# Router weights, value bias and the fourth batch's rows at other places in the head of the first attention

## The reference, cut to what matters

```python
# x (8, 100, 512), context (8, 722, 512) of which the causal mask leaves the first 100 rows
q = layernorm(x) @ q_w + q_b
k = context @ k_w + k_b
v = context @ v_w + v_b                      # 16 heads of 32
y = softmax(mask(q k^T / sqrt(32))) v
x = x + y @ o_w + o_b
# router of the first experts, on layernorm(layernorm(x)) * gamma + beta
logits = xf @ Wg.T + bg                      # 8 experts
```

## Time and profile before

| | us |
|---|---|
| median of 3 runs | 1704.23 |
| lowest, highest | 1703.96, 1705.78 |
| the profiled execution, its own time | 1707.12 |
| span of the profiled execution | 1705.4 |
| PE busy in the span | 1587.5 (93%) |
| DVE, ACT, POOL busy | 1133.0, 821.1, 262.7 |

### The profile page before, as it was taken

How to read it: one execution, slowest core, us unless ns; L and a number is a source line. 1 busy time by engine, 2 the same in 40 slices (tenths; PEclk the granted TensorE clock), 3 DMA queues, 4 the chain that set the end, 5 groups by cost and what they waited for, 6 DMA issues and landing times.

```text
span 1705.4 us, 32823 instructions
## 1 busy us (share of the span) xinstructions
PE 1587.5 (93%) x12252; PEld 1398.6 (82%) x12252; DVE 1133.0 (66%) x2066; ACT 821.1 (48%) x1542; POOL 262.7 (15%) x301
## 2 busy tenths in 40 slices
PE   6999699999999699899999999999999869999992
PEld 5787499999999589689888888888888669999991
DVE  3688667777777552367676766767676677776774
ACT  2444355555555332256555554646464434444442
POOL 1112201000000130011111111111111141111213
PEclk9999799999999899999999999999999979999996
DMA  6997366666666534231120111120203046656653
GB/s 188 363 400 255 110 225 228 218 213 204 221 205 215 146 134 174 100 107 37 33 55 24 52 28 48 28 60 20 60 16 100 19 145 220 212 182 217 228 194 89
DMA packets 93595, 246.06 MB, mean 144 GB/s; under 512 B 32646, under 2 KB 39302, under 8 KB 78390
## 3 DMA queue, kind: packets, MB, share of 16 engines
q1 hardware_dynamic: 84278, 223.15, 38.4%
q0 software_dynamic: 9216, 21.53, 5.5%
HBM read 179.14 MB, written 65.50 MB: 143 GB/s over the span
## 4 chain that ended last, share of the span: by engine, by line
PE 49%; DVE 4%; DMA 2%; ACT 1%; issue 1%; SPq 0%; POOL 0%; DVEq 0%; POOLq 0%; ACTq 0%
PE banks L2031 13%; PE banks L1164 10%; PE banks L2092 5%; PE banks L1141 5%; PE banks L2076 4%; PE banks L2065 4%; PE banks L2106 3%; PE banks L2052 3%; DMA token_sums<-e_y,e_dest 1%; DMA a_bo<-bo 1%; PE banks L1133 1%; ACT a_P L2364 0%; DVE a_nmax L2231 0%; DVE a_cl L2209 0%; DVE x_res L1446 0%
## 5 line engine op out<-in xcount | busy, mean ns | idle before, releaser
L2031 PE MATMUL banks<-a_ch,a_wm 128*128 128x362 f32 (+1 forms) x1024 | 284.6, 339 | 5.3 <-DVE a_cl L2209 5.3
L1217 DVE TENSOR_TENSOR e_lo<-e_raw,e_hi 128x2048 fp32r<-128x2048 f32 x97 | 224.4, 2313 | 53.1 <-ACT e_hi L1301 50.7
L1164 PE MATMUL banks<-e_xh,e_hi 128*128 128x256 f32 x768 | 216.6, 282 | 0.0
L1164 PE MATMUL banks<-e_xl,e_hi 128*128 128x256 f32 x768 | 216.1, 281 | 0.0
L1164 PE MATMUL banks<-e_xh,e_lo 128*128 128x256 f32 x768 | 215.8, 281 | 0.0
L1301 ACT CAST e_hi<-e_raw 128x2048 fp32r<-128x2048 f32 x98 | 185.9, 1905 | 13.4 <-PE banks L1141 13.4
L2031 PEld LDWEIGHTS banks<-a_ch,a_wm 128*128 128x128 f32 x1024 | 185.3, 189 | 6.7 <-DVE a_cl L2209 6.4
L2031 PE MATMUL banks<-a_cl,a_wm 128*128 128x362 f32 (+1 forms) x512 | 168.4, 329 | 0.0
L1112 POOL DMA_INDIRECT token_sums<-e_y,e_dest x32 | 76.9, 2404 | 580.8 <-DVE e_y L1274 321.8
L1141 PE MATMUL banks<-e_hi,e_hh 128*128 128x512 f32 x384 | 152.8, 398 | 0.0
L1164 PEld LDWEIGHTS banks<-e_xh,e_hi 128*128 128x128 f32 x768 | 145.2, 189 | 7.7 <-DVE e_lo L1217 2.1
(11 more groups left out here) (296 smaller groups left out, 3351.2 us busy)
## 6 DMA issues: line engine op xcount, KB each, us to landing
e_raw<-wout SPq DMA_DIRECT2D x50, 1024.0 KB, 15.3
e_raw<-w SPq DMA_DIRECT2D x34, 1024.0 KB, 22.0
slot_rows<-a_zero SPq DMA_DIRECT2D x66, 514.0 KB, 10.1
e_raw<-wgate SPq DMA_DIRECT2D x17, 1024.0 KB, 4.9
e_raw<-wup SPq DMA_DIRECT2D x17, 1024.0 KB, 5.5
a_craw<-ctxT SPq DMA_DIRECT2D x32, 361.0 KB
e_xs<-slot_rows SPq DMA_DIRECT2D x9, 514.0 KB, 7.0
a_craw<-slot_rows SPq DMA_DIRECT2D x9, 514.0 KB
```

Of the source, the lines that this page charges most:

```text
L1164: mm = nc.tensor.matmul(ps[:, bank, 0:CAP], w[:, cc, cut], x[:, cc, :], start=t == 0, stop=t == len(terms) - 1)
L1217: nc.vector.tensor_tensor(lo[g % 2][i], raw[q % RAW][:], hi[g % 2][i].bitcast(F32), ALU.subtract)\
L2031: mm = nc.tensor.matmul(ps[:, 6 + half, 0:wide], w[:, cc, cut], x[:, cc, start:start + wide], start=cc == 0 and t == 0, stop=cc == DC - 1 ...
```

## The change

The router's two scalings (`wgg`, `wgb`) move from DVE's head, ahead of the rows of x(2), to the end of the head, and the spreading of the value bias moves from turn 0 to just ahead of them. The router bias product moves from PE's head to turn 0, behind `values(0)` and ahead of the value bias product, and goes to bank 5 instead of bank 3. Its addition on DVE moves to turn 0, where `vb_wide` was made. The rows of x(3) move from behind the addition to `ob` to ahead of `weights_low(2)`. PE's wait for `lbs` (the addition done) moves from `scores(0)` to the value bias product, which uses the same bank 5. Nothing is added or left out.

```diff
--- before.py
+++ after.py
@@ -533,7 +533,6 @@
                         pe.wait_ge(rx, b - 1)
                     if b == 0:
                         pe.wait_ge(rounded, 2)
-                        pe.wait_ge(lbs, 1)
                     cut = slice(T * i, T * i + T)
                     for q in range(4):
                         nc.tensor.matmul(ps[0:T, q, 0:4 * T], ident_r[:], mask_r[:].rearrange("p f t -> p (f t)"),
@@ -623,10 +622,6 @@
                 turn_x(1, 5)
                 project_half(0, "q", 0)
                 project_half(0, "q", 1)
-                pe.wait_ge(wgs, 1)
-                for cc in range(DC):
-                    mm = nc.tensor.matmul(ps[0:T, 3, 0:E], ones[:], wgb[:, cc, :], start=cc == 0, stop=cc == DC - 1)
-                mm.then_inc(lbm, 1)
                 pe.wait_ge(xts, 2)
                 turn_x(2, 5)
                 pe.wait_ge(pjs, 1)
@@ -644,9 +639,14 @@
                         idle_products(6, wo[0])
                     values(b)
                     if b == 0:
+                        pe.wait_ge(xts, 3)
+                        pe.wait_ge(wgs, 1)
+                        for cc in range(DC):
+                            mm = nc.tensor.matmul(ps[0:T, 5, 0:E], ones[:], wgb[:, cc, :], start=cc == 0, stop=cc == DC - 1)
+                        mm.then_inc(lbm, 1)
                         pe.wait_ge(vbw, 1)
                         pe.wait_ge(w_in["o"], 16)
-                        pe.wait_ge(xts, 3)
+                        pe.wait_ge(lbs, 1)
                         for cc in range(DC):
                             mm = nc.tensor.matmul(ps[0:T, 5, :], vb_wide[:, cc, :], w["o"][:, cc, :],
                                                   start=cc == 0, stop=cc == DC - 1)
@@ -798,14 +798,9 @@
                 normalise_rows(0)
                 normalise_rows(1)
                 input_stats(2)
-                dve.wait_ge(g_in, 64)
-                own.note(nc.vector.tensor_tensor(wgg[:], wg[:], bc(gam[:], E), ALU.mult))
-                nc.vector.tensor_tensor(wgb[:], wg[:], bc(bet[:], E), ALU.mult).then_inc(wgs, 1)
                 normalise_rows(2)
                 projected(0, "q", 0)
                 projected(0, "q", 1)
-                dve.wait_ge(lbm, 1)
-                nc.vector.tensor_tensor(lbias[:], ps[0:T, 3, 0:E], bg[:], ALU.add).then_inc(lbs, 1)
                 context_low(0)
                 projected(0, "k", 0)
                 projected(0, "k", 1)
@@ -815,6 +810,11 @@
                 dve.wait_ge(made, 4 + r.CONSTANTS)
                 nc.vector.tensor_copy(rows[:, :, D], r.ids[:]).then_inc(labelled, 1)
                 nc.vector.tensor_copy(rows2[:, :, D], r.ids[:, 0:COPIES]).then_inc(labelled, 1)
+                dve.wait_ge(c_in, 32)
+                nc.vector.tensor_copy(vb_wide[:], bc(vb[:], T)).then_inc(vbw, 1)
+                dve.wait_ge(g_in, 64)
+                own.note(nc.vector.tensor_tensor(wgg[:], wg[:], bc(gam[:], E), ALU.mult))
+                nc.vector.tensor_tensor(wgb[:], wg[:], bc(bet[:], E), ALU.mult).then_inc(wgs, 1)
                 for b in range(B):
                     if b >= 1:
                         scaled(b - 1)
@@ -830,8 +830,9 @@
                     if b >= 2:
                         route_best(b - 2)
                     if b == 0:
-                        dve.wait_ge(c_in, 32)
-                        nc.vector.tensor_copy(vb_wide[:], bc(vb[:], T)).then_inc(vbw, 1)
+                        dve.wait_ge(lbm, 1)
+                        nc.vector.tensor_tensor(lbias[:], ps[0:T, 5, 0:E], bg[:], ALU.add).then_inc(lbs, 1)
+                        normalise_rows(3)
                         weights_low(2, wo, "o")
                         dve.wait_ge(obm, 1)
                         nc.vector.tensor_tensor(ob[:], ob[:], ps[0:T, 5, :], ALU.add).then_inc(obs, 1)
@@ -839,8 +840,6 @@
                         add_output(b - 1)
                     if b >= 2:
                         route_slot(b - 2)
-                    if b == 0:
-                        normalise_rows(3)
                     if b >= 1:
                         route_rows(b - 1)
                     if block_at(b):
```

## The result

| | before | changed |
|---|---|---|
| median of 4 runs, us | 1705.01 | 1694.57 |
| lowest, highest, us | 1703.96, 1707.67 | 1691.33, 1696.38 |
| profiled execution, its own time, us | 1707.12 | 1696.38 |
| its span, us | 1705.4 | 1694.6 |
| PE busy in the span, us | 1587.5 | 1584.1 |

The ratio is 0.9933, with an interval of 0.9917 to 0.995 (95%).

What follows compares the result with a forecast made beforehand. PE, busy 93% of the span, was taken as the bound, each early idle stretch paid again in slow matmuls. Gains of 7.8 + 3.3 + 1.8 = 12.9 us off 1704.23 gave 1691.3 us, range 1688.5 to 1698.0.

Steps and rivals of the forecast that it cites:

- (a): Head: without the router steps, x(2)'s rows and the keys come earlier; keys end at 23.75 against 31.92, 8.2 us earlier.
- (b): Between keys and maximum: `vb_wide` and two scalings add some 0.5 us; maximum starts at 29.1, 7.7 us earlier.
- (c): Turn 0, router product behind the values: value bias product starts at 33.75, 7.8 us earlier; the product costs nothing more.
- (d): Turn 0, rows of x(3) ahead of o_w's low half: PE's 3.30 us idle goes, `turn_x(3)` starts at 37.4.
- (e): From `turn_x(3)` to `attended(0)`: without slow clock 4.45 us against 6.2, gaining 1.8 us; `attended(0)` starts at 41.85.
- The sum: Total gain by `attended(0)`: 7.8 + 3.3 + 1.8 = 12.9 us, with the later stages moving as a block.
- At no cost: Edits costed at nothing: earlier context and zero stores, and POOL's additions of `ob` beside DVE's last key bias and first reciprocal.
- the 1.1 us of the range's end: Upper cost allowed for POOL's additions of `ob` beside DVE work; taken as 0, at 1.1 the sum is 11.8 us.
- The stores of zeros: Stores come 8.3 us earlier, the work 12.9; the first scatter should not wait for them, otherwise the gain falls to 8.3.
- A: Rival: next wait sits closer, ACT or `obs` could set turn 0; gain 6 to 11 us, 1693 to 1698; chance 0.15.
- B: Rival: other loads held the head anyway, or a later stage had slack; gain under 3.4 us; chance 0.05.
- C: Rival: PE stays at the slow clock through the head, 18 to 42 us; 6.1 us slower, 1710.3; chance 0.04.

Runs made afterwards that it cites:

- bank7_again: The kernel of bank7 (changed kernel, router product in bank 7) run once more on another chip: 1703.3 us, ratio 0.991 to the kernel before.
- head_only: Changed kernel with the rows of x(3) put back behind the addition to `ob`: 1699.67 us, ratio 0.9949 to the kernel before.
- product_in_head: Changed kernel with router product back ahead of PE's keys, scalings and addition back in DVE's head behind x(2)'s rows and query biases: 1703.99 us, ratio 0.9965 to before.
- rows3_only: Kernel before with only the rows of x(3) moved ahead of o_w's low half: 1702.97 us, ratio 0.9966 to the kernel before.
- bank7: Changed kernel with router product in bank 7, PE's `lbs` wait moved behind the value bias product: four runs 1691.62 to 1697.84 us, ratio 0.9919 to before.

## Why the prediction was right

**(a) and (b), the head.** The keys ended at 18.29 + 5.68 = 23.97 (23.75 forecast) and the maximum started at 29.34 (29.1). Both are late by the same 0.2 us, since the statistics of x(2), and with them everything, came 0.4 us later in this execution (16.39 against 16.01).

**(c), the meeting behind the values.** The value bias product started at 34.20, within the ends 33.65 to 34.4 and 0.45 behind my 33.75. It was luck in part: the context of pair 1 came 0.4 us past the late end that I had allowed (27.4 against 27.0), and the router product ran at the full clock (0.79 us), where that end had it at 1.50. One sentence of (c) was wrong, that the moved product costs nothing more since PE would wait for DVE anyway. `vb_wide` is ready early now; what PE waits for is the read of bank 5, which the move itself brought in, and without it `attended(0)` comes 1.1 us earlier (bank7_again). Head_only measured (a) to (c) by themselves: 8.7 us by the ratio, for a sum of 7.8. product_in_head showed that DVE's part alone does not give it.

**(d), the rows of x(3).** `turn_x(3)` started at 37.68 with no idle before it, as forecast (37.4). What had held its rows was more than the order of DVE's work: DVE stood 3.54 us for ACT's high half of o_w ahead of them, a wait that the forecast counts in its time for `obs` and does not name.

**(e), the clock.** From there to `attended(0)` it took 42.23 - 37.68 = 4.55 us (4.45 forecast). Against the 6.2 of before that is 1.7 us, for 1.8 forecast; but head_only, with an idle stretch of nearly the same length, paid 3.3. This term is no constant; in the tail the stretch at 0.50 differed between executions behind one and the same wait. rows3_only measured (d) and (e) together: 5.8 us by the ratio for 5.1.

**The sum** was 12.9 to `attended(0)`; the profile shows 12.5, and 13.1 at the experts. By terms that is 7.3 us for 7.8, 3.5 for 3.3 and 1.7 for 1.8. The first comparison gave 11.4 us by the ratio (8.5 to 14.2), the two later ones 0.9915 each, 14.5 us; the intervals hold 12.9 each time. The shortfall of the first profiled pair lies, as far as its profiled execution shows it, in the second attention's tail, which the forecast treated as part of a block that only moves. Execution by execution its length varies by 5 us. That is a spread that my range had put down to the scatter of runs, without a cause.

**At no cost.** Of the two DVE steps that I had put beside POOL's additions of `ob` (41.06 to 43.56) only the key bias ran there, with its usual 0.57 us; the reciprocal started at 43.87, after them. In bank7_again the reciprocal ran 1.0 us beside them (from 42.40) and took its 2.66 us all the same. So the 1.1 us of the range's end did not occur. L767, which reads two SBUF inputs, was slow again beside such an addition (1.25 us). The Trainium skill, GPSIMD Engine Reference, in its table of properties, names VectorE instructions with two SBUF inputs as those that contend with GpSimd; the trace agrees, for L767 on the one side and for the key bias and the reciprocal, which read PSUM, on the other. The stores of zeros went unnoticed too: the first scatter stood at 129.25 for its own issue (0.24 us), as in the earlier trace rows.

**The rivals.** A would have shown `attended(0)` held by `obs`, or a gain of 6 to 11 us; `obs` was there at 40.46 (40.2 forecast), 1.8 us ahead, and repeated runs gave 14.5. DVE's 3.1 us for ACT's high half of o_w lie ahead of that point and are in it. The first median alone, 10.4, would have fitted A's time: only the points in the profile and the repetition tell them apart. B asked for a gain under 3.4 us, C for a clock of 0.50 between 18 and 42 us; it was 1.00. One argument against B was wrong as written: not every load is issued anew behind the barrier, since SP issued weights of the experts at 130.39 in the kernel before, within the first stage. They moved to 122.42, and the first expert matmul had the whole gain.

## What to carry to other kernels

Where an engine stands for a load whose result is needed much later, look at every engine in whose queue that product stands: moving it on VectorE alone showed no gain in the time here, and with TensorE's product moved too the head gave some 8 us. Give a moved product a bank of its own where one is free: the wait that came with the shared one cost 1.1 us, which the profile shows and the time of the whole does not. Price a stop of TensorE twice, for itself and for the slow matmuls behind it, and take the second as a range and not as a number. When a measured gain falls short, compare the two traces at points that both programs have before looking for a flaw in the change: here the missing part had gone some 1300 us behind it, in a stretch that was the same in both.

## What the runs showed of the hardware

- **The clock's return varies.** After one and the same wait of 2.64 us the granted clock stood at 0.50 for 3.4 us in one execution of the kernel before and for 13.6 us in another, and for 3.4, 6.8 and 17.1 us in three of the changed kernel. In ten profiles with that wait the second attention's tail took 30.2 to 35.4 us; in the three with the wait filled it took 28.7 each time. I had taken what follows a fixed wait to be a fixed cost.
- **One execution ran at less than half speed.** The profiled execution of bank7 took 3999.07 us, its other four 1691.62 to 1697.84. Its mean granted clock is given as 1.000, yet the keys took twice and more what they should:

```profile
25.30 15.14 PE L522 MATMUL banks<-a_ctx,e_raw 128*128 128x200 f32 x32
```

  That is 15.14 us for 5.68 at full clock and for 7.34 half of it slow; DVE's and ACT's durations were the usual ones (a maximum of 1.82 us). What held TensorE back there, the profile does not say, and it did not come again in bank7_again.
- **Sets of runs differ by nearly what the change is worth.** The kernel before took 1705.01, 1708.8, 1709.49 and 1717.62 us in its four sets of runs, a spread of 12.6 us, while the ratio of the change was 0.9933 in the first of them and 0.9915 in both others where it was timed.
